# A gated cross-attention block: group 0's softmax denominators move to ScalarE, and four neighbours move

## The reference

```
q = relu(layernorm(x)); k = v = relu(ctx)              # per head
p = softmax(q k^T / sqrt(32)) ; o = p v                 # 256 x 256 per head
x = x + tanh(g_xattn) * relu(o W_x^T + b)
n = layernorm(x); xr = mu_r n + (1 - mu_r) prev(n); xk = mu_k n + (1 - mu_k) prev(n)   # prev: the token before
x = x + tanh(g_ffn) * sigmoid(xr W_r^T) * (relu(xk W_k^T)^2 W_v^T)
```

## Time and profile before

| | |
|---|---|
| median of three runs | 2754.9 us |
| the profiled execution | 2759.9 us, span 2758.1 us, granted TensorE clock 0.989 |
| TensorE busy | 2652.6 us, 96% of the span |
| VectorE, ScalarE, GpSimd busy | 2298.3, 1693.7, 1105.1 us |
| chain that ended last | TensorE 91%, DMA 4%, VectorE 2% |
| denominators on TensorE (L1002) | 3072 matmuls, 206.6 us |
| spreading transposes (L1012) | 128, 24.4 us |
| VectorE: reciprocal L764, copy L762, tensor_scalar L800 | mean 1751, 409, 657 ns |
| ScalarE: relu_v L483 (768 and 256 columns), k_halve L503 | 837, 418, 1051 ns |
| GpSimd: o_low L366, xr_low L392, square L399 | mean 1302, 2398, 1046 ns |
| SP: issue of the four x loads | 2.89 us |
| DMA | 576.7 MB, mean 209 GB/s |

### The profile page before, as it was taken

The page is one execution under the profiler, slowest core; times in us unless marked ns, Lnnn a source line. Parts: engine busy times, 40 slices in busy tenths (PEclk is TensorE's granted clock), DMA queues, the critical chain, the costliest instruction groups (busy, mean ns, idle before and its releaser), DMA issues.

```text
span 2758.1 us, 65460 instructions
## 1 busy us (share of the span) xinstructions
PE 2652.6 (96%) x20354; PEld 2059.1 (75%) x20354; DVE 2298.3 (83%) x4109; ACT 1693.7 (61%) x3531; POOL 1105.1 (40%) x902
## 2 busy tenths in 40 slices
PE   2699999999999999999999999999999999999998
PEld 1477777777777777777777777777777777777776
DVE  3687888888888888888888888888888888888864
ACT  2465566666666666666666666666666666666652
POOL 0144344344344444444434434434434444444433
PEclk9799999999999999999999999999999999999999
DMA  7676777777777777777777777777777777777641
GB/s 220 175 218 191 211 217 209 224 220 208 222 226 212 213 229 215 209 233 217 205 229 224 205 229 218 209 225 221 208 221 228 209 214 231 213 209 234 204 119 44
DMA packets 507775, 576.71 MB, mean 209 GB/s; under 512 B 175824, under 2 KB 407248, under 8 KB 507728
## 3 DMA queue, kind: packets, MB, share of 16 engines
q1 hardware_dynamic: 355152, 341.18, 42.3%
q10 hardware_dynamic: 152576, 234.93, 28.6%
HBM read 373.56 MB, written 201.33 MB: 208 GB/s over the span
## 4 chain that ended last, share of the span: by engine, by line
PE 91%; DMA 4%; DVE 2%; SPq 2%; issue 1%; ACT 1%; POOL 0%; ACTq 0%; DVEq 0%; POOLq 0%
PE bank L1019 51%; PE bank L964 9%; PE bank L976 9%; PE bank L990 9%; PE bank L1002 7%; PE bank L948 3%; PE bank L931 2%; DMA o_mv<-o_dram 2%; PE bank L939 1%; DMA q_st<-m_t 1%; DMA o_dram<-o_val 1%; DVE o_val L764 1%; PE bank L1012 0%; SPq L296 0%; DVE m_nat L742 0%
## 5 line engine op out<-in xcount | busy, mean ns | idle before, releaser
L514 ACT ACTIVATE probs<-bank 128x512 f32<-128x512 f32 x1024 | 605.0, 597 | 547.3 <-PE bank L976 500.5
L742 DVE TENSOR_REDUCE m_nat<-bank 128x2 fp32r<-128x512 f32 x1024 | 687.6, 682 | 109.4 <-PE bank L964 109.1
L976 PE MATMUL bank<-q_st,k_st 97*128 97x256 f32 x2048 | 427.2, 290 | 27.8 <-DMA q_st<-m_t 27.7
L964 PE MATMUL bank<-k_st,q_st 96*128 96x256 f32 x2048 | 438.6, 296 | 14.7 <-ACT bank L526 6.3
L976 PEld LDWEIGHTS bank<-q_st,k_st 97*128 97x128 f32 x2048 | 358.2, 192 | 106.0 <-DMA q_st<-m_t 28.9
L964 PEld LDWEIGHTS bank<-k_st,q_st 96*128 96x128 f32 x2048 | 359.5, 193 | 77.7 <-ACT bank L526 17.1
L764 DVE RECIPROCAL o_val<-bank 128x256 f32<-128x256 f32 x192 | 336.2, 1751 | 60.0 <-PE bank L1002 56.6
L366 POOL TENSOR_TENSOR o_lo<-o_mv,o_hi 128x512 fp32r<-128x512 f32 x128 | 166.7, 1302 | 447.8 <-ACT o_hi L535 440.9
L526 ACT ACTIVATE bank<-bank,m_nat 128x256 f32<-128x256 f32 x512 | 227.6, 445 | 186.6 <-DVE m_nat L742 186.5
L399 POOL TENSOR_TENSOR xm<-xm 128x512 f32<-128x512 f32 x128 | 133.8, 1046 | 412.8 <-ACT xm L572 412.7
L1019 PE MATMUL bank<-xk_hi,w_hi 128*128 128x256 f32 x1024 | 296.4, 289 | 0.0
(11 more groups left out here) (94 smaller groups left out, 6088.2 us busy)
## 6 DMA issues: line engine op xcount, KB each, us to landing
q_st<-q_dram ACTq DMA_DIRECT2D x256, 256.0 KB, 4.8
k_st<-k_dram SPq DMA_DIRECT2D x256, 256.0 KB, 4.2
x_ln<-x_dram SPq DMA_DIRECT2D x256, 128.0 KB
k_raw<-ctx_t_dram SPq DMA_DIRECT2D x256, 128.0 KB, 4.9
q_dram<-q_high ACTq DMA_DIRECT2D x64, 512.0 KB, 3.0
q_dram<-q_raw ACTq DMA_DIRECT2D x64, 512.0 KB, 4.1
k_dram<-k_high SPq DMA_DIRECT2D x64, 512.0 KB, 4.4
k_dram<-k_raw SPq DMA_DIRECT2D x64, 512.0 KB, 5.5
```

The source lines that it names most:

```text
L514: nc.scalar.activation(probs[:, n // GR % 2, n % GR, :, :].rearrange("p v t -> p (v t)"), st_bank[n % 2][:, :], ACT.Exp).then_inc(exp_read ...
L742: nc.vector.tensor_reduce(m_nat[:, c % 2, n % GR, :], s_bank[n % 2][:, :].rearrange("p (u y) -> p u y", u=NU), AX_X, ALU.max, negate=True) ...
L964: mm = nc.tensor.matmul(s_bank[n % 2][:, T * u:T * u + T], q_st[0:QK, c, g, P * u:P * u + P], k_st[0:QK, c, g, :], start=True, stop=True)
L976: mm = nc.tensor.matmul(st_bank[n % 2][:, T * v:T * v + T], k_st[0:ST, c, g, P * v:P * v + P], q_st[0:ST, c, g, :], start=True, stop=True)
```

## The change

Groups 0 and 1 (SUMMED = 2) get their denominators from ScalarE's accumulator. `den` has room for both groups; sum_exp(i + 1, 0 to 3) stand in steps 10 to 13 of ScalarE and sum 4 moves from 13 to 14; `invert(i, 0)` stands on VectorE after head_max(8); TensorE's denominators(i, 0) become turn_rden(i, 0); norm_o of group 0 copies. Scores 2 to 5 wait for the sums of heads 0 to 3 instead of their maxima. k_halve moves from step 10 to step 7 of ScalarE, write_q from step 13 to step 14 behind sum 4. relu_v goes to VectorE, after invert(i, 1) and after head_max(13). x's rows are loaded with a pattern of one stride (row 4r + m to partition r of block m), and o_mv is read with a stride of 4 elements in place of runs of 16.

```diff
--- before.py
+++ after.py
@@ -39,7 +39,7 @@
     KC = D // P
     GR = P // HD
     CH = HEADS // GR
-    SUMMED = 1
+    SUMMED = 2
     assert NU == 2 and KC == 4 and GR == 4 and CH == 4 and HD == 32
     QK = 3 * HD
     ST = QK + 1
@@ -74,7 +74,7 @@
         q_st = sb("q_st", [P, CH, GR, T], F32R)
         probs = sb("probs", [P, 2, GR, NU, T])
         o_val = sb("o_val", [P, 2, T])
-        den = sb("den", [P, GR * NU])
+        den = sb("den", [P, SUMMED, GR * NU])
         rden = sb("rden", [P, GR * NU])
         o_mv = sb("o_mv", [P, 2 * GR, T // GR])
         o_hi = sb("o_hi", [P, KC, T], F32R)
@@ -242,7 +242,7 @@
                     for m in range(GR):
                         part = slice(P // 2 * (m % 2), P // 2 * (m % 2) + P // 2)
                         sp.dma_start(x_ln[part, m // 2, :],
-                                     x[b].rearrange("(a k m) d -> m k a d", k=KC, m=GR)[m]).then_inc(x_loaded, 16)
+                                     x[b].rearrange("(r m) d -> m r d", m=GR)[m]).then_inc(x_loaded, 16)
 
             def load_k(b):
 
@@ -363,7 +363,7 @@
                     pool.wait_ge(o_hi_ready, NU * b + u + 1)
 
                     after(pool, z_ready, NU * (b - 1) + u + 1)
-                    nc.gpsimd.tensor_tensor(by_tile(o_lo, u), o_mv[:, :, :].rearrange("p g (k a) -> p k g a", k=KC),
+                    nc.gpsimd.tensor_tensor(by_tile(o_lo, u), o_mv[:, :, :].rearrange("p g (a k) -> p k g a", k=KC),
                                             by_tile(o_hi, u).bitcast(F32), ALU.subtract).then_inc(o_lo_ready, 1)
 
             def x_diff(b, u):
@@ -477,12 +477,6 @@
                     act.dma_start(q_st[HD:QK, c, :, :].bitcast(F32),
                                   q_dram[par, c].rearrange("h f g t -> (h f) g t")).then_inc(q_stacked[c], 16)
 
-            def relu_v(b, part):
-                if on(b):
-                    act.wait_ge(v_loaded[part], 16 * (b + 1))
-                    nc.scalar.activation(v_pos[:, :, v_cols[part]], v_pos[:, :, v_cols[part]],
-                                         ACT.Relu).then_inc(v_ready, 1)
-
             def q_copy(b, u):
                 if on(b):
                     act.wait_ge(q_turned, NU * b + u + 1)
@@ -518,21 +512,21 @@
 
                 if on(b):
                     act.wait_ge(s_maxed, HEADS * b + n + 1)
-                    g = n % GR
+                    c, g = n // GR, n % GR
                     if g == 0:
-                        after(act, rsum_ready, b)
+                        after(act, rsum_ready, SUMMED * (b - 1) + c + 1)
                     for u in range(NU):
                         scores = s_bank[n % 2][:, T * u:T * u + T]
                         last = nc.scalar.activation(scores, scores, ACT.Exp,
-                                                    bias=m_nat[:, SUMMED % 2, g, u:u + 1].bitcast(F32),
-                                                    accum_out=den[:, NU * g + u:NU * g + u + 1])
+                                                    bias=m_nat[:, c % 2, g, u:u + 1].bitcast(F32),
+                                                    accum_out=den[:, c, NU * g + u:NU * g + u + 1])
                     last.then_inc(s_summed, 1)
 
             def o_high(b, u):
                 if on(b):
                     act.wait_ge(o_moved, 16 * GR * (NU * b + u + 1))
                     after(act, z_ready, NU * (b - 1) + u + 1)
-                    nc.scalar.activation(by_tile(o_hi, u), o_mv[:, :, :].rearrange("p g (k a) -> p k g a", k=KC),
+                    nc.scalar.activation(by_tile(o_hi, u), o_mv[:, :, :].rearrange("p g (a k) -> p k g a", k=KC),
                                          ACT.Copy).then_inc(o_hi_ready, 1)
 
             def z_relu(b, u):
@@ -616,7 +610,6 @@
                 split_high(i, 3)
 
                 exponent(i, 3)
-                relu_v(i, 0)
                 stack_q(i + 1, 0, 1 - par)
 
                 exponent(i, 4)
@@ -636,6 +629,7 @@
 
                 exponent(i, 7)
                 stack_q(i + 1, 1, 1 - par)
+                k_halve(i + 2)
                 split_high(i, 6)
 
                 exponent(i, 8)
@@ -650,24 +644,26 @@
                 q_halve(i + 2)
 
                 exponent(i, 10)
+                sum_exp(i + 1, 0)
                 r_tanh(i - 2, 0)
                 xt_copy(i - 1, 1)
-                k_halve(i + 2)
 
                 exponent(i, 11)
-                relu_v(i, 1)
+                sum_exp(i + 1, 1)
                 stack_q(i + 1, 2, 1 - par)
 
                 exponent(i, 12)
+                sum_exp(i + 1, 2)
                 xk_high(i - 1, 0)
                 r_tanh(i - 2, 1)
 
                 exponent(i, 13)
+                sum_exp(i + 1, 3)
+                xk_high(i - 1, 1)
+
+                exponent(i, 14)
+                sum_exp(i + 1, 4)
                 write_q(i + 2, par)
-                xk_high(i - 1, 1)
-                sum_exp(i + 1, 4)
-
-                exponent(i, 14)
                 load_v(i + 1, 0)
 
                 exponent(i, 15)
@@ -719,6 +715,12 @@
                                                 mv[:, 0, u, 0:1], rstd[:, 0, u:u + 1],
                                                 ALU.subtract, ALU.mult).then_inc(x_normed, 1)
 
+            def relu_v(b, part):
+                if on(b):
+                    dve.wait_ge(v_loaded[part], 16 * (b + 1))
+                    nc.vector.tensor_scalar(v_pos[:, :, v_cols[part]], v_pos[:, :, v_cols[part]],
+                                            0.0, None, ALU.max).then_inc(v_ready, 1)
+
             def q_low(b):
                 if on(b):
                     dve.wait_ge(q_hi_ready, b + 1)
@@ -758,7 +760,7 @@
                     if c % 2 == 1:
 
                         after(dve, o_lo_ready, NU * b + c // 2)
-                    if c == SUMMED:
+                    if c < SUMMED:
                         nc.vector.tensor_copy(o_val[:, c % 2, :], pv_bank[:, T:2 * T]).then_inc(rden_ready, 1)
                     else:
                         nc.vector.reciprocal(o_val[:, c % 2, :], pv_bank[:, T:2 * T]).then_inc(rden_ready, 1)
@@ -766,15 +768,16 @@
                     nc.vector.tensor_tensor(o_val[:, c % 2, :], pv_bank[:, 0:T], o_val[:, c % 2, :],
                                             ALU.mult).then_inc(o_ready, 1)
 
-            def invert(b):
-
-                if on(b):
-                    dve.wait_ge(s_summed, GR * (b + 1))
-                    nc.vector.reciprocal(rden[:, :], den[:, :]).then_inc(rsum_ready, 1)
-                    dve.wait_ge(rsum_ready, b + 1)
-
-                    after(dve, o_written[SUMMED % 2], 16 * 2 * b)
-                    nc.vector.tensor_copy(o_val[:, SUMMED % 2, :].rearrange("p (u g f) -> p u g f", u=NU, g=GR),
+            def invert(b, c):
+
+                if on(b):
+                    dve.wait_ge(s_summed, GR * (SUMMED * b + c + 1))
+                    after(dve, rsum_spread, SUMMED * b + c)
+                    nc.vector.reciprocal(rden[:, :], den[:, c, :]).then_inc(rsum_ready, 1)
+                    dve.wait_ge(rsum_ready, SUMMED * b + c + 1)
+
+                    after(dve, o_written[c % 2], 16 * 2 * b)
+                    nc.vector.tensor_copy(o_val[:, c % 2, :].rearrange("p (u g f) -> p u g f", u=NU, g=GR),
                                           rden[:, :].rearrange("p (g u a) -> p u g a", u=NU, a=1
                                                                ).broadcast_to([P, NU, GR, HD])).then_inc(rsum_spread, 1)
 
@@ -840,13 +843,15 @@
                 split_low(i, 0)
 
                 head_max(i, 8)
+                invert(i, 0)
                 split_low(i, 1)
 
                 head_max(i, 9)
                 stats_1(i + 2)
 
                 head_max(i, 10)
-                invert(i)
+                invert(i, 1)
+                relu_v(i, 0)
                 split_low(i, 2)
 
                 head_max(i, 11)
@@ -859,6 +864,7 @@
                 norm_o(i, 0)
 
                 head_max(i, 13)
+                relu_v(i, 1)
 
                 head_max(i, 14)
                 add_x(i - 1, 0, 1 - par)
@@ -956,8 +962,8 @@
                     if g == 0:
                         pe.wait_ge(q_stacked[c], 32 * (b + 1))
                         pe.wait_ge(k_stacked[c], 32 * (b + 1))
-                    if SUMMED * GR <= n - 2 < SUMMED * GR + GR:
-                        pe.wait_ge(s_summed, GR * b + n - 1 - SUMMED * GR)
+                    if 0 <= n - 2 < SUMMED * GR:
+                        pe.wait_ge(s_summed, SUMMED * GR * b + n - 1)
                     else:
                         after(pe, s_maxed, HEADS * b + n - 1)
                     for u in range(NU):
@@ -1003,13 +1009,13 @@
                                                   moving, start=(n == 0), stop=(n == len(sums) - 1))
                     mm.then_inc(pv_ready, 1)
 
-            def turn_rden(b):
-
-                if on(b):
-                    pe.wait_ge(rsum_spread, b + 1)
-                    after(pe, o_ready, CH * b + SUMMED)
```

(11 more changed lines are left out.)

## The result

The changed kernel took 3081.9 us (3078.6 to 3090.8, 4 runs), the kernel before 2754.5 beside it: ratio 1.1195, 95% interval 1.1178 to 1.1212. The forecast was 2722 with a range up to 2862.

The account below looks back on a forecast made before the run. TensorE's issued work was taken as the bound (busy 2324.2 of 2333.0 us mid-stretch). Per batch -0.98 - 0.40 + 0.80 = -0.58 us, times 57 = 33 off 2754.9: 2722 us, range 2686 to 2862.

Parts of the forecast that it names:

- TensorE's part: Group 0's 16 denominator matmuls go, two transposes come: 0.98 us saved per batch, 56 us over 57.
- k_low: VectorE's k_low starts before GpSimd's xk_low and isn't held up: 0.40 us gained per batch, bounds 0 and 0.43.
- the clean rival: VectorE comes in time, copied-maxima stall only 0.2 us: -1.18 per batch, 2688 us; chance 0.15.
- ScalarE's part: Four more exponential pairs fit ScalarE's waiting before scores 3, by 0.2 us: no cost, at most 0.3 us per batch.
- x's rows and o_mv: One-stride x loads and strided o_mv reading: cost 0, bounds -0.1 to 0.3 us per copy.
- q's write, later: q's 1 MB write moves beside other transfers; delay to group 3's output hidden by 0.3 to 1.1 us cover: 0.
- rival 2: q's write delays group 3's output; projection stalls 2.7 to 3.5 us per batch for o_low: about 2845 us; chance 0.30.
- VectorE's part: Relu (0.8 us) and extra inversion delay group 2's copied maxima; TensorE stalls 0.80 us per batch at q's first turn.
- rival 3: Relu comes behind GpSimd's square, norm_1 behind o_low: stall 2 to 3 us at q's turn, about 2820 us; chance 0.10.
- the one that the forecast is wrong: Sign: TensorE's middle-stretch idle time grows by over 80 us, or scores 2 to 5 wait for ScalarE's sums.

Follow-up runs that it names:

- e1: Kernel before plus group 0's sums on ScalarE and k's upper half in step 7, 40 one-column copies ahead of ScalarE's loop: 2709.6 us, 0.9827.
- c2: Changed kernel with q's write back in step 13, both relus back on ScalarE, 40 one-column copies ahead of ScalarE's loop: 2727.8 us, 0.9897.
- b2: Changed kernel with q's write back in step 13 and 40 one-column copies ahead of ScalarE's loop: 2899.5 us, 1.0559.
- d1: Changed kernel with only 40 one-column copies added ahead of ScalarE's loop: 3022.4 us, 1.0965.
- c1: Changed kernel with q's write back in step 13 and both relus back on ScalarE, no copies ahead of the loop: 2943.9 us, 1.0676.
- d4: Kernel before plus group 0's sums on ScalarE and one-stride rows, k_halve still after exponent 10, 40 copies ahead of ScalarE's loop: 2771.6 us, 1.0062.
- a4: Kernel before with only q's write moved from step 13 to step 14 of ScalarE: 2949.0 us, 1.0690.
- a1: Kernel before with sixteen one-column copies added in each of ScalarE's iterations: 2756.9 us, 0.9994.
- d2: Kernel before with 80 one-column copies ahead of ScalarE's loop: 2758.1 us, 1.0001.
- b3: Kernel before with only the one-stride rows of x and o_mv read accordingly: 2746.7 us, 0.9972.
- d3: Kernel before with only group 0's sums moved to ScalarE's accumulator, plus 40 one-column copies ahead of ScalarE's loop: 2761.2 us, 1.0020.

## Why the prediction was wrong

The runs make a ladder, each step one part of the change (the first has two), no fetching up to its last:

| kernel | median, us | step |
|---|---|---|
| before | 2754.5 | |
| e1: sums, k's upper half in step 7 | 2709.6 | -45 |
| c2: and one-stride rows | 2727.8 | +18 |
| b2: and relu on VectorE | 2899.5 | +172 |
| d1: and q's write in step 14 | 3022.4 | +123 |
| changed kernel (loop fetched again) | 3081.9 | +59 |

The steps hold in this order only: the rows alone gave -7, the relu alone +1, the write alone +193, and the fetching 216 between c1 and c2. These stalls cover one another, so no row of the table is that part's share of the 327 us; the relu's is not, as said below.

- **TensorE's part, -0.98 per batch.** Right to 0.1: 1.50 - 0.60 = 0.90 in e1. The last 0.10, which the shifted scores were to gain, didn't come (0.34 us to the next start before, 0.37 in e1).
- **k_low, -0.40.** Right in mechanism: 1.20 us in the mean of all 64, in the changed kernel too (before: 1.94). There k_low starts 0.65 us ahead of xk_low; before, 0.2 behind it. The size is less sure. Both terms make 1.38; the period of e1 fell by 1.1, from 41.0 to 39.9, near the sum of the clean rival (1.18). Beside TensorE's 0.90 that leaves 0.2 for k_low, and no run has it alone.
- **ScalarE's part, 0 with a bound of 0.3.** It fits only because k's upper half moved. d4 less c2 is 44 us, 0.8 per batch, over the bound: I asked what the move costs and not what staying would.
- **x's rows and o_mv, 0, bounds -0.1 to 0.3 per copy.** The copy lost 0.5, outside the bounds; on the path that was 18 us in e1's company.
- **The step that failed: "q's write, later ... I take the added delay as within it".** It was priced at 0 and cost 193 us alone (a4), 3.4 per batch, within the 2.7 to 3.5 that rival 2 gave the stall. The mechanism was written down with its place and its point of decision; I chose the cover of 0.3 to 1.1 us against a stretch whose share was already 1.03. And I priced only o_low: in a4 the late write also holds up the sums and the maxima's row, by 1.1 and 1.0 us each time. Rival 2's total (2845) was still too low: with no fetching the changed kernel takes 3022 (d1), over the top of my range as well.
- **VectorE's part, "I take 0.8" for the relu and 0.80 for the stall.** Not what failed in the changed kernel, and not right either. The larger relu took 0.59 us there, the stall of 0.80 per batch is 7.0 us in all, and the second half of norm_1 starts 0.3 or some 3.8 us ahead of o_low and takes 0.72. The term was too dear by some 40 us, which the other losses hide. The meetings of rival 3 come where q's write is early: in b2 the relu took 1.40 beside the square and norm_1's second half came behind o_low, 2.1 us of stall in 61 turns, 172 us in all. The late write makes o_low late and so seems to keep it from meeting norm_1. No run has the late write with the relu on ScalarE, so what the relu costs in the changed kernel is not known.
- **What no step had: the code.** I counted ScalarE's instructions by their time and not by the room they take. Its fetching is 59 us of the 327 on top of the late write and the relu, and 216 where neither is there (c1, c2).
- **A wait can cost more than itself.** b2's 131 us of waiting stand beside 172 us of time. Behind the wait that ends at 1401.67 TensorE's granted clock is 0.73 over 6.3 us (windows of b2, below). Over the whole execution it is 0.966 in b2 and 0.989 in c2. It is 0.953 in d1, with 64 waits of 2.7 us, but 0.987 in a4, whose three waits are of 1.0 to 1.3 us. How the 172 us divide between idle time and clock no run separates.

```profile
1399.30:1401.60 2.30, 0.48 (x5) 0.28 (x3) 2.30 (x4) 1.63 (x3) 2.30 (x2) 1.00 1.01 309
1401.70:1408.00 6.30, 6.30 (x27) 5.38 (x28) 2.85 (x6) 2.53 (x4) 1.32 (x1) 0.73 0.48 135
```

Of the signs that the prediction named, rival 2's came (waits for o_low, ScalarE 3 us and more at o_mv). So did the one that the forecast is wrong, TensorE's idle time in the middle stretch: it grew by 194 us, not by 80. The other, scores 2 to 5 waiting for ScalarE's sums, came only five times (7.5 us).

**What stays open.** Which places of the loop are bad. Counted in records of ScalarE (good to a few records), loops of 288 to 295 that start at 429, 430 or 438 are fetched again; of 289 to 295 at 458, 469, 470 and 478 not; nor of 251 to 257 at 346, 358 and 438. All of these, and the 5 packets a round, would follow if code came in units of 128 records, a loop that touches four units fetched the four and one ahead, and a loop that touches three stayed. That was fitted afterwards, with the place of the units' edges free, and no run tested it at a place chosen to refute it. Open too is why d1 loses 268 us, where the write alone loses 193 and everything else but the relu gains 27 (c2). The relu on VectorE or the lost cover of the denominators could make up the rest.

## What to carry to other kernels

Where a stretch's transfers already fill the queues, a large write moved into it is paid by whoever reads back behind it: price it at the full time of its bytes, and look for every reader. Work moved to another engine costs what it meets there: look for the neighbour that it slows (GpSimd here), and ask what stood in front of the victim that the same change removes. After adding instructions to a looped engine look at the instruction queue's packets on the profile's page first: a period that alternates with the loop's halves, with "issue" at the jump, is code being fetched, and may hide the verdict on everything else.

## What the runs showed of the hardware

- A loop of some 290 records on ScalarE is fetched again in each round or not, by its place: 216 us with the same work (c1, c2), a gap of 4 to 7 us at each jump where it is fetched; sixteen copies a batch or 80 copies ahead of the loop cost nothing themselves (a1, d2).
- The copy of 128x512 with a stride of four elements in the source takes ScalarE 1.13 us in place of 0.63 (means of b3 and of the kernel before), and GpSimd's subtraction 1.56 in place of 1.33 (means of d4 and d3).
- Behind waits of TensorE of 2.68 us (changed kernel) and 1.89 us (b2) the granted clock, 1.00 before them, averages 0.52 over 6.8 us and 0.73 over 6.3 us.
